# Attention: the probabilities' halves transposed by DMA from SyncE in place of TensorE, value products one unit later

## The reference, cut to what matters

```python
q = rmsnorm((hidden @ q_proj_w.T) per head, q_norm_w)
k = rmsnorm(repeat((ctx @ k_proj_w.T) per head, 4), k_norm_w)
v = repeat((ctx @ v_proj_w.T) per head, 4)
scores = einsum('bhqd,bhkd->bhqk', q, k) / sqrt(128) + attention_mask
attn = softmax(scores, axis=-1)
out = einsum('bhqk,bhkd->bhqd', attn, v)
return out.reshape(B, Q, 32 * 128) @ o_proj_w.T
```

## Times and profile before

| | |
|---|---|
| Three runs | 737.06 us, 734.94 us, 737.27 us; median 737.06 us |
| Profiled execution, first to last instruction (span) | 734.7 us |
| TensorE (PE) busy | 694.5 us, 95% |
| VectorE (DVE) busy | 455.9 us, 62% |
| ScalarE (ACT) busy | 408.6 us, 56% |
| GpSimd (POOL) busy | 398.2 us, 54% |
| Mean granted TensorE clock | 0.981 |
| DMA | 49.48 MB, mean 67 GB/s |

### The profile page before, as it was taken

The page is one execution under the profiler, slowest core; times in us unless marked ns, Lnnn a source line. Parts: engine busy times, 40 slices in busy tenths (PEclk is TensorE's granted clock), DMA queues, the critical chain, the costliest instruction groups (busy, mean ns, idle before and its releaser), DMA issues.

```text
span 734.7 us, 14040 instructions
## 1 busy us (share of the span) xinstructions
PE 694.5 (95%) x4380; PEld 358.6 (49%) x4380; DVE 455.9 (62%) x1086; ACT 408.6 (56%) x834; POOL 398.2 (54%) x438
## 2 busy tenths in 40 slices
PE   6649999999999999999989999999999999999997
PEld 2224445444444444555545555555555555444453
DVE  5999876444344347444458888888888884000484
ACT  4425466433343326777777777777777775214222
POOL 4723234345455432786868666666666665339201
PEclk9959999999999999999999999999999999999999
DMA  8702000443444330322130000000000000234001
GB/s 335 310 0 72 1 0 0 128 133 128 143 128 132 110 110 35 115 62 111 59 112 2 1 1 0 0 0 0 0 0 0 0 0 11 106 115 165 8 1 58
DMA packets 13944, 49.48 MB, mean 67 GB/s; under 512 B 1594, under 2 KB 1722, under 8 KB 10973
## 3 DMA queue, kind: packets, MB, share of 16 engines
q1 hardware_dynamic: 11122, 44.33, 17.3%
q10 hardware_dynamic: 2795, 4.79, 2.2%
HBM read 48.03 MB, written 1.09 MB: 67 GB/s over the span
## 4 chain that ended last, share of the span: by engine, by line
PE 69%; DVE 13%; POOL 7%; issue 7%; ACT 2%; DMA 1%; SPq 0%; POOLq 0%; DVEq 0%; ACTq 0%
PE ps L264 21%; PE ps L266 20%; PE ps L265 20%; PE ps L342 9%; POOL wsp L1014 3%; POOL hlr L1014 3%; DVE st L1137 1%; DVE nw L1149 1%; DVE nw L1148 1%; DVE f32r L1153 1%; DMA stage<-in_first_chunks 1%; DVE xT L1211 1%; DVE nw L1150 1%; PE ps L497 1%; DVE hlr L1236 0%
## 5 line engine op out<-in xcount | busy, mean ns | idle before, releaser
L1014 POOL TENSOR_TENSOR wsp<-stage,wsp 128x512 f16<-128x512 f32 (+1 forms) x93 | 135.2, 1477 | 129.2 <-ACT wsp L735 68.5
L342 PEld LDWEIGHTS ps<-ident,hlr 128*128 128x128 f16 x1536 | 100.9, 98 | 51.5 <-POOL hlr L1014 3.9
L342 PE MATMUL ps<-ident,hlr 128*128 128x128 f16 x1536 | 117.3, 220 | 5.0 <-ACT q_sb L827 2.0
L896 ACT ACTIVATE f32r<-f32r,mneg 128x512 f32<-128x512 f32 x128 | 92.4, 722 | 49.5 <-DVE mneg L1375 49.1
L1014 POOL TENSOR_TENSOR hlr<-f32r,hlr 128x512 f16<-128x512 f32 x52 | 61.1, 1176 | 100.1 <-ACT hlr L787 66.5
L1093 POOL TENSOR_SCALAR rinv<-rinv 128x1 f32<-128x1 f32 x128 | 72.9, 569 | 71.6 <-issue 69.0
L1375 DVE CUSTOM_DVE_ANT_0 f32r<-ps,nmask 128x512 f32<-128x512 f32 x128 | 88.0, 688 | 30.9 <-issue 17.8
L1384 DVE SCALAR_TENSOR_TENSOR hlr<-f32r,rinv,hlr 128x512 f16<-128x512 f32 x128 | 93.9, 733 | 1.5 <-POOL hlr L1094 1.0
L1094 POOL TENSOR_SCALAR hlr<-f32r,rinv 128x512 f16<-128x512 f32 x128 | 88.4, 690 | 0.0
L1294 DVE TENSOR_REDUCE ss<-f32r 128x4 f32<-128x512 f32 x48 | 32.9, 685 | 55.1 <-ACT f32r L776 54.9
L264 PE MATMUL ps<-q_sb 128*128 128x512 f16 x128 | 49.4, 386 | 9.0 <-POOL q_sb L1014 7.3
(11 more groups left out here) (224 smaller groups left out, 1461.7 us busy)
## 6 DMA issues: line engine op xcount, KB each, us to landing
stage<-in_moe SPq DMA_DIRECT2D x18, 512.0 KB, 3.7
stage<-in_wq SPq DMA_DIRECT2D x8, 1024.0 KB, 4.7
stage<-in_wo SPq DMA_DIRECT2D x8, 1024.0 KB, 4.8
stage<-in_moe SPq DMA_DIRECT2D x18, 256.0 KB, 3.3
hlr<-gates_dram ACTq DMA_DIRECT2D x18, 256.0 KB, 3.2
k_sb<-in_wkv SPq DMA_DIRECT2D x3, 1024.0 KB, 18.5
stage<-in_first_chunks SPq DMA_DIRECT2D x4, 512.0 KB, 5.4
q_sb<-in_ctx_nat SPq DMA_DIRECT2D x1, 2048.0 KB, 14.9
```

The source lines that it names most:

```text
L342: last = pe.transpose(dst.bitcast(F16)[:, at:at + P], src_hi_lo[:, l, c * P:(c + 1) * P], ident[:, :])
L896: act.activation(f32r[:, j % 4, :], f32r[:, j % 4, :], ACT.Exp, bias=mneg[:, j % 4:j % 4 + 1], scale=-1.0, accum_out=psum_col[:, j % 4:j % ...
L1014: return pool.tensor_tensor(dst_lo, src, dst_hi, ALU.subtract)
```

## The change

The transposes of the probabilities leave TensorE. For each tile SP waits for `s_pl` (both halves are written) and issues one transposing DMA of the whole slot of `hlr` (128 partitions by 1024 fp16 values, 256 KB) straight into `pT` in SBUF; each slot has a completion semaphore, `s_pT[j % 4]`. `prob_transposes` and `prob_copy` are gone. `pT` has four buffers, one for each m: slot 1 of `wsp`, `xT`, `pT1` and the new `pT2`. The values of a unit are made three iterations of m behind its scores, in place of two, and o_hi and o_lo move by one too. POOL's `prob_hi` waits for the landing of the slot's earlier DMA, and so does DVE's `prob_lo`. `s_ol` starts at 1, by an increment on the mask's scaling.

```diff
-        pT0 = xT
-        pT = [pT0, pT1]
+        pT2 = sb("pT2", [P, 4, 2, GW], F16)
+        pT = [wsp[:, 1, :, :].rearrange("p a b -> p (a b)").rearrange("p (h l c) -> p h l c", h=REP, l=2), xT, pT1, pT2]
...
+        s_pT = [sem(f"s_pT{h}") for h in range(REP)]
...
-            with sp.Fori(0, KVH // 2) as i:
-                for s in range(2):
-                    sp.wait_ge(s_wql, 4 * (KVH + 2 * i + s - 1))
-                    load(s, wo[2 * i + s], WG)
+            for n in range(3):
+                sp.wait_ge(s_wql, 4 * (KVH + n - 1))
+                load(n % 2, wo[n], WG)
+
+            def prob_transpose(j, split):
+
+                slot = j % 4
+                sp.wait_ge(s_nl, 16 + NT * KVH)
+                sp.wait_ge(s_pl, split)
+                sp.dma_start_transpose(pT[j // REP][:, slot, :, :].rearrange("p l (c q) -> p (l c) q", c=SC),
+                                       hlr[:, slot, :, :].rearrange("p l x -> p (l x)")).then_inc(s_pT[slot], 16)
+
+            for j in range(4 * REP):
+                prob_transpose(j, j + 1)
+            with sp.Fori(1, KVH) as g:
+                for j in range(4 * REP):
+                    prob_transpose(j, sp.to_reg(16 * g + j + 1))
+            for n in range(3, KVH):
+                sp.wait_ge(s_wql, 4 * (KVH + n - 1))
+                load(n % 2, wo[n], WG)
...
-            def prob_transposes(j, k, wait_bank=True):
-                pe.wait_ge(s_pl, k + 1)
-                if wait_bank:
-                    pe.wait_ge(s_Tc, k - 1)
-                transposes(hlr[:, j % 4, :, :], ps[4 + j % 2][:, :], hi_lo_major).then_inc(s_T, 1)
-
...
-                    pe.wait_ge(s_Tc, 4 * w + 4)
+                    for h in range(REP):
+                        pe.wait_ge(s_pT[h], 16 * (w + 1))
                     if wait_bank:
-                        pe.wait_ge(s_ol, w - 1)
+                        pe.wait_ge(s_ol, w)
...
-                    [pT[par][:, :, l, c * P:(c + 1) * P] for l in range(2)], c == 0, c == SC - 1)
+                    [pT[mw][:, :, l, c * P:(c + 1) * P] for l in range(2)], c == 0, c == SC - 1)
...
                         scores(g, j, k, first)
-                        prob_transposes(j, k - 4, not first or j >= 6)
-                    if not first or m >= 2:
-                        values(4 * g + m - 2, g if m >= 2 else g - 1, (m - 2) % 4, c, not first)
+                    if not first or m >= 3:
+                        values(4 * g + m - 3, g if m >= 3 else g - 1, (m - 3) % 4, c, not first)
...
-            for j in range(4):
-                prob_transposes(j, 16 * KVH - 4 + j)
-                values(4 * KVH - 2, KVH - 1, 2, j)
+            for w in (1, 2):
+                for c in range(SC):
+                    values(4 * (KVH - 1) + w, KVH - 1, w, c)
...
-            def prob_copy(j, k, u, wait_values):
-                act.wait_ge(s_T, k + 1)
-                if wait_values:
-                    act.wait_ge(s_pv, u - 1)
-                act.copy(words(pT[(j // REP) % 2][:, j % REP, :, :]), ps[4 + j % 2][:, :]
-                         .rearrange("p (l w) -> p l w", l=2)).then_inc(s_Tc, 1)
-
...
-                    if not first or j >= 4:
-                        prob_copy((j - 4) % 16, k - 4, 4 * g + m - 1, hh == 0 and (not first or m >= 3))
-                    if hh == 0 and (not first or m >= 3):
-                        o_hi(4 * g + m - 3, (m - 3) % 4)
+                    if hh == 0 and not first:
+                        o_hi(4 * g + m - 4, m)
...
-                    pool.wait_ge(s_T, freed)
+                    pool.wait_ge(s_pT[j], freed)
...
-            dve.tensor_scalar(nmask[:, :, :], nmask[:, :, :], -8.0, None, ALU.mult)
+            dve.tensor_scalar(nmask[:, :, :], nmask[:, :, :], -8.0, None, ALU.mult).then_inc(s_ol, 1)
...
-            def prob_lo(j, k):
+            def prob_lo(j, k, earlier=None):
                 dve.wait_ge(s_ph, k + 1)
+                if earlier is not None:
+                    dve.wait_ge(s_pT[j % 4], 16 * earlier)
...
-                        prob_lo((j - 2) % 4, k - 2)
-                    if hh == 1 and (not first or m >= 3):
-                        o_lo(4 * g + m - 3, (m - 3) % 4)
+                        prob_lo((j - 2) % 4, k - 2, None if first and j < 6 else 4 * g + (j - 2) // REP)
+                    if hh == 1 and not first:
+                        o_lo(4 * g + m - 4, m)
...
-            for m in range(3):
-                o_lo(4 * KVH - 3 + m, (m + 1) % 4)
+            for m in range(4):
+                o_lo(4 * KVH - 4 + m, m)
...
-    nc = bacc.Bacc("TRN2", target_bir_lowering=False, num_devices=1)
+    nc = bacc.Bacc("TRN2", target_bir_lowering=False, num_devices=1, dynamic_dma_scratch_size=1024)
```

More of the change, by code:

```diff
@@ L228, in xattn_ffn_kernel @@
         s_pl = sem("s_pl")
-        s_T = sem("s_T")
-        s_Tc = sem("s_Tc")
         s_pv = sem("s_pv")
+        s_pT = [sem(f"s_pT{h}") for h in range(REP)]
         s_oh = sem("s_oh")
@@ L633, in _ @@
             pe.wait_ge(s_wql, 4 * (2 * KVH))
-            pe.wait_ge(s_ol, 4 * KVH)
+            pe.wait_ge(s_ol, 1 + 4 * KVH)
             for t in range(NT):
@@ L926, in _ @@
                 attention(g, False)
+            o_hi(4 * KVH - 4, 0)
             o_hi(4 * KVH - 3, 1)
-            for j in range(4):
-                prob_copy(12 + j, 16 * KVH - 4 + j, 4 * KVH - 1, j == 0)
             o_hi(4 * KVH - 2, 0)
@@ L1085, in prob_hi @@
             def prob_hi(j, k, first):
-                summed, freed = k + 1, k - 3
+                summed, freed = k + 1, 4 * (k - j)
                 if not first:
@@ L1408, in _ @@
             inverse_sum(3, end - 1)
-            prob_lo(2, end - 2)
-            prob_lo(3, end - 1)
-            for m in range(3):
-                o_lo(4 * KVH - 3 + m, (m + 1) % 4)
+            prob_lo(2, end - 2, 4 * KVH - 1)
+            prob_lo(3, end - 1, 4 * KVH - 1)
+            for m in range(4):
+                o_lo(4 * KVH - 4 + m, m)
             dve.wait_ge(s_lw, 2)
```

## The result

The changed kernel takes **715.9 us** in the median of four runs (714.5 to 718.5); the kernel before takes 736.2 us in the median of its four. The ratio is 0.9729, with a 95% interval of 0.9705 to 0.9753: 20 us faster. The forecast was 718.0. The profiled execution took 715.52 us, its span is 713.7 us, against 734.7 before.

The account below looks back on a forecast made before the run. TensorE was taken to bound the attention loop, with DVE next. From the profiled 734.7 us, a gain of 20.6 and a loss of 1.5 gave 715.6, plus 2.4 to the median 718.0; range 713 to 775, the forecast's own 713 to 726.

Parts of the forecast that it names:

- PE was the bound and DVE the next: Attention loop: PE alone sets 1.80 us a tile; without transposes it needs 1.30, and DVE bounds at 1.64.
- The step: Masked scores, tile 2 to 127: 1.52 us in group 0, 1.643 in the loop, 204.0 us against 224.6, gain 20.6.
- Where the gain comes from: Loop: PE loses transposes of 0.44 us a tile and its wait for ACT's copy; gain 20.6 us.
- (a) Pace: Transposing DMAs: 1.1 us a slot on the DMA engines, SP's issue 0.33 if like a copy's, both under 1.64.
- this rival: SP or the DMA path takes longer than a step per transposing DMA, deciding from 1.80 us on; chance 0.10.
- (b) Landing: Loop over four `hlr` slots: 4 x step = 2.3 + landing; landing 3.7 us, hidden up to 4.3.
- The rivals that hung on it: Landing of 4.3 to 4.9 us hidden in part, 730 us, chance 0.13; longer landing becomes the bound, 770, chance 0.18.
- POOL's and DVE's new waits, the lag: Loop: DVE's wait costs nothing beyond POOL's; values a unit later leave four steps, 6.6 us, over any landing.
- The end: Before the output projection: values(30) wait for unit 28's o_lo, now behind the last two prob_lo; loss 1.5 us.
- The clock: Loop: PE idles a fifth of each step and its granted clock might fall to 1.2 GHz, +100 us; chance 0.02.

Follow-up runs that it names:

- pe_four: Changed kernel plus four unused identity transposes per tile on PE behind the scores: 717.1 us, ratio 0.9724 to the kernel before.
- pe_eight: Changed kernel plus eight unused identity transposes per tile on PE behind the scores: 724.6 us, ratio 0.9839 to the kernel before.
- short_out: Changed kernel with DVE's o_lo writing 16 columns in place of 512, result not full: 704.6 us, ratio 0.9566 to the kernel before.
- lag_alone: Kernel before with four buffers and values one unit later, transposes still on PE and copies on ACT: 728.2 us, ratio 0.9890.
- split_dma: Changed kernel moving each slot by two transposing DMAs of 128 KB, one per half: 849.1 us, ratio 1.1532 to the kernel before.
- pair_dma: Changed kernel with one transposing DMA of 512 KB for two tiles: 756.4 us, ratio 1.0273 to the kernel before.
- three_slots: Changed kernel where POOL waits for the landing of tile k-3 in place of k-4: 735.3 us, ratio 0.9985 to the kernel before.
- lag_two: Changed kernel with values two units behind the scores, as before the change, DMAs and four buffers kept: 718.9 us, ratio 0.9754.
- early_out: Changed kernel with the o_lo of unit 28 moved ahead of the last inverse sum and last two low halves: 713.0 us, ratio 0.9681.
- pe_corrects: Changed kernel with o_lo taken off DVE: PE adds one correcting matmul a unit and ACT writes the low half: 699.7 us, ratio 0.9506.

## Why the prediction was right, step by step

**PE was the bound and DVE the next.** Right as to PE: pe_four shows that it has slack, pe_eight that its old load brings back 1.74 us a tile. Right in the main as to DVE: short_out shows that the step follows it, 11 us for 14 taken off. What the prediction passed over is POOL, which it put at 1.25 us a tile and so far from the step: POOL's two operations take 1.38 us here, and in 52 of 74 tiles DVE's low half starts only when POOL's high half ends.

**The step.** Forecast 1.52 in group 0 and 1.643 in the loop, 204.0 us for the 125 steps; measured 201.6. With group 0 and the first step as forecast the loop's is (201.6 - 1.8 - 18.2) / 112 = 1.62. The size is right to 1.3%, and that is in part luck. The prediction took 1.54 us for a step in which DVE doesn't wait. But in that step the low half starts at

```profile
486.62 0.73 DVE L1384 SCALAR_TENSOR_TENSOR hlr<-f32r,rinv,hlr 128x512 f16<-128x512 f32 x1
```

and the next masked scores at 487.48, 0.86 us later, where it is 0.65 to 0.67 when nothing holds them (483.36 to 484.01 in the changed kernel). So 0.2 us of the 1.54 were a wait for scores, too short to be listed, and DVE's own step is 1.33. With three of 1.33 and one of 1.95 the loop would step at 1.49, if DVE alone set it. It doesn't, since most tiles wait some 0.17 us for POOL's high half; that wait, which the prediction didn't have, took the place of the one that it had without seeing it. The step with an o_lo came out longer too (2.08 in the mean, forecast 1.95), and the other three shorter (1.47, forecast 1.54). The gain was 23.05, forecast 20.6; this term makes nearly all of the 2 us between 718.0 and 715.9.

**Where the gain comes from.** The sum was right, its wording too simple. It gave all to the transposes and copies leaving, the end of PE's wait for the copy among it, and took the later value products only as cover for the landings. lag_alone gives 8 of the 20 us with all transposes in place, since the wait for ACT's copy (1.80 - 1.74 a step) goes with it.

**(a) Pace.** Mis-sized in both parts, and harmless here by luck, not by the sum. "SP's issue, 0.33 us for a copy, is nothing beside that, if a transpose's is alike": it isn't, 1.23 us. The DMA engines' time was forecast at 1.1 us a tile and is 1.38; the pieces are of 256 bytes as guessed, but 21 ns each and not 17. Both lie under 1.61 by 0.38 and 0.23 us; split_dma and pair_dma show what it is to lose that. For SP's hold the prediction named a rule of the Trainium skill, of the page "DMA: Bandwidth & Descriptors", in the table under "Why a DMA increments its semaphore by 16 and not by 1", an estimate of 1.7 us for 64 tiles. The measured 1.23 us is under it, and at half the tiles it is 1.23 again, where the rule by its wording would halve: the trace agrees that the hold is far over a copy's, not that it goes by the tile. The 261 GB/s of the same page's section "Latency and other measured facts" were an estimate of 1.0 us a slot; 256 KB in 1.38 us are 190 GB/s, so the trace stays under that figure. What held this rival off is that one DMA carries a slot.

**(b) Landing.** Forecast 3.7 us, hidden up to 4.3; measured 3.2 and, by three_slots, 4.2. The turn was forecast at 2.3 us beside the landing and comes to 2.2. Right, and it kept 1.0 us in hand, not 0.6. The rivals that hung on it fell: POOL waits for no DMA in those 140 us.

**POOL's and DVE's new waits, the lag.** "Four steps, 6.6 us, over any landing": right, no wait for a landing in the loop. In lag_two, with one unit less, such waits appear. What the text didn't foresee is PE's wait for o_lo, 23.5 us in 140, since it counted o_lo's move only for the end. Slack took it.

**The end.** Forecast 7.56 us from the last masked scores to the output projection, measured 7.80; forecast loss 1.5, measured 1.8. early_out shows the named cause.

**The clock.** Granted 1.00 through the loop, with PE at 82%. Right. The 0.86 that the rival rested on the earlier trace rows doesn't go with the load by itself: in the same 384 to 388 us of the changed kernel PE is busy 2.01 of 4 us again, and the granted clock is 1.00.

## What to carry to other kernels

When an engine at 95% loses a quarter of its work, the gain is the distance to the next engine, and that is read from the places where the next one doesn't wait. Look there for short waits that no view lists, by comparing starts with a place where nothing holds the engine, ask which engine the freed one will wait for next, and average over the whole pattern, here four tiles, not over two steps. A transposing DMA takes work off TensorE at a price per DMA on the issuing queue and a price per small piece on the DMA engines: compare both with the step before cutting or joining transfers, and count the buffers in the loop that its landing closes. After such a change look for the engine with new slack and give it work from the new bound, as pe_corrects does.

## What the runs showed of the hardware that was not expected

- A transposing DMA from SBUF to SBUF holds SP's queue 1.23 us at 128 KB and at 256 KB and some 1.9 us at 512 KB; it lands 2.5, 3.2 and 4.3 us after its issue.
- It moves pieces of 256 bytes, at 21 ns each here and 19 ns in split_dma (48,482 packets, 48.1% of 16 engines in 120 us). At 21 ns 16 engines together would move 190 GB/s. In pe_corrects the engines reach a share of 0.93 at 176 GB/s, and the landing rises only to 3.4 us.
- TensorE's granted clock stayed 1.00 with PE busy 82% of 140 us. It was 0.94 in pair_dma, with PE busy 91.0 of 120 us, and 0.83 in split_dma with 77.8 of 120, where some matmuls of 634 ns in place of 379 stand among the rows, the lower level. PE waits in both for much of the stretch, for DVE and for landings, so I don't take the clock for what paces them; that wasn't tried by itself.
- POOL's two operations on a tile take 0.67 + 0.72 = 1.38 us, where they took 0.57 + 0.69 = 1.25, with nothing changed in them. In pe_corrects they take 0.52 + 0.84. What stretches them was not tried.
